# The attention sums of a convolution chain: k stationary in two column halves of the array, put together by one matmul with two identities

## The chip, the cores and the metric

The kernel runs on one core of a Trainium2 chip. The metric is the device time of one execution in microseconds (us), measured over several runs. The kernel is written in a low-level language in which every engine has its own program: TensorE (PE, with its weight loads listed as PEld), VectorE (DVE), ScalarE (ACT), GpSimd (POOL) and SyncE (SP, which issues all DMAs). The programs meet at semaphores. All numbers here are fp32; operands typed F32R are fp32 that TensorE takes in a faster, less exact way. A plain fp32 matmul appears in the trace as two pairs of weight load and matmul; an F32R matmul and a transpose appear as one.

## What is computed

The input x is (8, 64, 64, 48): eight images of 4096 tokens with 48 channels. Four layers follow one another. Only the first has attention, and only its middle is touched here:

```python
xn = (xe - bn_mean) * (bn_gamma * rsqrt(bn_var + BN_EPS)) + bn_beta
q, k, v = split(xn @ w_qkv + b_qkv, 3, axis=2)
q = q - mean(q, axis=2); k = k - mean(k, axis=2)
q2, k2 = q * q, k * k
q2 = _l2n(q2 / (sum(q2, axis=2) + 1e-07), axis=2)
k2 = _l2n(k2 / (sum(k2, axis=2) + 1e-07), axis=1)
kv = einsum('bnc,bnd->bcd', k2, v)
t2 = einsum('bnc,bcd->bnd', q2, kv) / sqrt(N)
attn = (v + t2) @ w_ln + b_ln
```

Then come a 1x1 convolution over attn and the shortcut, a 3x3 convolution (conv2) and a 1x1 convolution (w3), a depthwise and pointwise layer (L1), a layer of mixed experts with its own depthwise convolution (expand, taps, project), and another depthwise and pointwise layer (L3).

## The kernel before

**The attention sums.** v is linear in x, so the kernel never forms kv from v. For each image it forms one matrix over the 4096 tokens, G = [x, k2, 1]' k2, with 97 rows (48 of x, 48 of k2, one of ones) and 48 columns. The rows of x and of ones give kv after a small matmul with prepared weights; the diagonal of the k2 rows gives the norm of k2 over the tokens. The tokens lie in the tile `tok`, 128 partitions by 2 parities (even and odd image rows) by 16 runs by 145 columns (q, x, k, 1). `attention_sums` (L1017) makes 32 matmuls into one bank, over 2 parities and 16 runs, all accumulated: the stationary operand is the 97 columns x, k, 1 of a token group, the moving one its 48 columns of k. Each contracts over 128 tokens.

**What stands around it.** DVE's `sums_out` (L592) waits for `g_done` and copies G to `gt`, and G times a diagonal mask to `gm`. PE's `attention_weights` (L1028) waits for both, and makes two small matmuls (L1032, L1033). From these DVE and ACT make the weights `w1_cur` of conv1 (`conv1_weights`, L599). Before the sums, ACT squares the scores into `tok`, DVE's `norms_begin` (L567) sums the squares, and POOL's `scale_k` (L939) scales k in `tok`; `attention_sums` waits for that (`k_scaled`). DVE's `norms_end` (L582) scales q, and stands in DVE's program ahead of `sums_out`.

**The order of the work.** The images are staged in a software pipeline that is written out by hand: `iteration(f, attn, back)` works on conv2, L1 and the routing of image f, on the attention of image attn = f + 1, and on the project and L3 steps of image back = f - 1. It runs once for f = 0 (no back), in a loop for f = 1 to 6, and once for f = 7 (no attn). Image 0's attention stands ahead of all of them. So six images have their attention sums beside an L3 (f = 1 to 6), and images 0 and 1 have it without one. On PE the order in an iteration is: conv2, project and L1, attention scores (L1013), routing (L1103), l3 in four chunks of 15 matmuls of 512 columns (L1094, L1096, L1097), attention_sums (L1024), out_tokens (16 transposes, L1172), attention_weights, expand_halo (L1109, L1110), and conv1 with expand between its chunks (L1045, L1053, L1109).

`l3` (L1178) fills banks that ACT empties one after another (`l3_out`, L1359, into `outc`). `out_tokens` (L1165) waits for the last of these, and its own results go out through ACT (`tokens_out`, L1365). `expand_halo` (L1112) waits for the mixed weights of DVE's `mix_weights` and for the DMAs of `copy_x2`.

Of all this the change's steps touch `attention_sums`, `sums_out`, the call of `l3`, and the preparation on DVE (L442 to L461).

Of the kernel before, what the change touches and what calls it, by code (L numbers as in the profile page):

```python
# [7 lines left out]
ALU = mybir.AluOpType  # L8
# [4 lines left out]
IMAGES, H, W, C = 8, 64, 64, 48  # L13
# [5 lines left out]
RUN = W // WQ  # L19
# [8 lines left out]
PCHUNKS = HALF // BANK  # L28
ROWS = BANK // W

Q_AT, X_AT, K_AT, TOK = 0, C, 2 * C, 3 * C + 1
# [25 lines left out]
BEHIND = 128 - C2  # L57
APART = C2 - BEHIND

B_COPIES, WT_COPIES, X2_COPIES = 7, 16, 4  # L60
# [55 lines left out]
def conv_chain_kernel(nc, a, out):  # L116

    ctx = ExitStack()
    with ctx:
        def sb(name, shape, dt=F32):  # L120
            return ctx.enter_context(nc.sbuf_tensor(name, shape, dt))

        def sem(name):
            return ctx.enter_context(nc.semaphore(name))
# [32 lines left out]

        s1, s2, u, r = (sb(n, [128, k, 2 * RUN]) for n, k in (("s1", 2), ("s2", 1), ("u", 2), ("r", 1)))
        gt, gm = sb("gt", [SUMS, C]), sb("gm", [SUMS, C])
        rk = sb("rk", [C, 1])  # L160
# [72 lines left out]
        norm_q, norm_k = sem("norm_q"), sem("norm_k")  # L233
        u_ready, q_scaled, k_scaled = sem("u_ready"), sem("q_scaled"), sem("k_scaled")
        gt_ready, w1_ready = sem("gt_ready"), sem("w1_ready")
        xq_ready, y1_slope, y1_max, y1h_ready, y1l_ready, y1l_last = (
# [169 lines left out]
        def token(par, i, at, n):  # L406
            return tok[:, par, i, at:at + n]
# [20 lines left out]
        def _(dve):  # L428
# [21 lines left out]
            step(nc.vector.memset(xq[C2:C2 + 1, :, :], 1.0))  # L450
            step(nc.vector.memset(ones[:], 1.0))

            def fold_norm(inv, shift, gamma, mean, beta):
# [5 lines left out]

            dve.wait_ge(prep_pe, 1)  # L460
            step(nc.vector.tensor_copy(col0[:, :], banks[0][0:C2, 0:Z_ROWS]))  # L461
            step(nc.vector.tensor_scalar_add(inv96[:, L0:L0 + 1], col0[:, Z_VAR:Z_VAR + 1], BN_EPS), "variance")
# [129 lines left out]
            def sums_out(image):  # L592

                bank = ring_a.bank(A_G)
                dve.wait_ge(g_done, image + 1)
                nc.vector.tensor_copy(gt[:, :], bank[0:SUMS, 0:C]).then_inc(gt_ready, 1)
                nc.vector.tensor_tensor(gm[:, :], bank[0:SUMS, 0:C], gram_mask[:, :], ALU.mult).then_inc(gt_ready, 1)

# [361 lines left out]
        def _(pe):  # L960
# [56 lines left out]
            def attention_sums(image):  # L1017

                bank = ring_a.take(pe, image, A_G)
                pe.wait_ge(k_scaled, image + 1)  # L1020
                for par in range(2):
                    for i in range(RUN):
                        first, final = par == 0 and i == 0, par == 1 and i == RUN - 1
                        last = nc.tensor.matmul(bank[0:SUMS, 0:C], token(par, i, X_AT, SUMS), token(par, i, K_AT, C),  # L1024
                                                start=first, stop=final)
                last.then_inc(g_done, 1)

# [149 lines left out]

            def l3(image):  # L1178
                pair_conv(image, L3, ring_d, D_L3, l3_done, range(PCHUNKS))

            def iteration(f, attn, back):
# [26 lines left out]
                if back is not None:  # L1208
                    l3(back)
                if attn is not None:  # L1210
                    attention_sums(attn)
                if back is not None:
                    out_tokens(back)
# [6 lines left out]
            attention_scores(0)  # L1220
            attention_sums(0)
            attention_weights(0)
            conv1(0, None)
# [7 lines left out]
            project(IMAGES - 1, range(PCHUNKS), last_image=True)  # L1231
            l3(IMAGES - 1)
            out_tokens(IMAGES - 1)
# [235 lines left out]
```

## Time and profile before

| what | us |
|---|---|
| median of 3 runs | 1265.95 (1265.3 to 1267.52) |
| the profiled execution's own time | 1266.09 |
| its span, first to last instruction | 1264.3 |
| PE busy with matmuls | 1175.6 (93% of the span) |
| PE busy with weight loads (beside the matmuls) | 756.8 (60%) |
| DVE busy | 892.4 (71%) |
| ACT busy | 475.6 (38%) |
| POOL busy | 119.8 (9%) |
| one iteration in the loop, from one image's sums to the next's | 142.2 |

The profiled execution lies 0.14 us above the median. A line of the views names the source line, the engine, the operation, the tile written and the tiles read, and the shape; for TensorE a form such as 128*97 128x48 is 128 rows by 97 stationary columns, and a moving operand of 128 partitions by 48 columns. PEclk is the clock granted to TensorE as a share of full speed. Matmul durations are modelled from start to the last result, and matmuls overlap, so the time that a row of them takes is read from their starts.

### The profile page before, as it was taken

Reading aid. Unit: us, or ns where it says so; the run is one execution under the profiler, and the core shown is the slowest. Engines: PE = TensorE matmul, PEld = TensorE weight load, DVE = VectorE, ACT = ScalarE, POOL = GpSimd, SP = SyncE. Lnnn points to the kernel's source line nnn. Section 1 sums busy time; section 2 is a strip of 40 time slices with the busy share of each in tenths; the row PEclk is TensorE's granted clock in tenths of the full one; section 3 lists DMA queues with packets and bytes.
Section 4 is the critical chain, followed back from the end, with each engine's and each line's share of the span. In section 5 each row is a group of like instructions: output and inputs, shape, how many; then the busy total and the mean of one; then the engine's idle time right before and its main releaser. Section 6 shows DMA issues by size and latency. Waiting matters only on the chain.

```text
span 1264.3 us, 14703 instructions
## 1 busy us (share of the span) xinstructions
PE 1175.6 (93%) x4981; PEld 756.8 (60%) x4981; DVE 892.4 (71%) x1154; ACT 475.6 (38%) x812; POOL 119.8 (9%) x72
## 2 busy tenths in 40 slices
PE   4789879999999999999999999999999999998986
PEld 3556566646665575656665575656665575655434
DVE  4552359984699459984699459984699459982850
ACT  3211334245532444245532444245532444242421
POOL 0310003000300003000300003000300003000000
PEclk9689869999999999999999999999999999999997
DMA  2011631069113772069113771069113770069016
GB/s 52 21 36 21 81 51 38 1 85 132 45 21 40 100 103 37 0 85 131 44 21 40 100 103 37 0 85 130 45 22 40 101 103 1 1 85 134 25 27 83
DMA packets 183179, 72.91 MB, mean 58 GB/s; under 512 B 174349, under 2 KB 174962, under 8 KB 183154
## 3 DMA queue, kind: packets, MB, share of 16 engines
q1 hardware_dynamic: 183154, 72.58, 41.6%
q8 instruction: 15, 0.25, 0.1%
q14 instruction: 10, 0.08, 0.0%
HBM read 10.51 MB, written 6.29 MB: 13 GB/s over the span
## 4 chain that ended last, share of the span: by engine, by line
PE 80%; DVE 7%; issue 4%; ACT 3%; SPq 2%; DMA 2%; POOL 0%; ACTq 0%; DVEq 0%; POOLq 0%
PE bank L1070 32%; PE bank L1094 8%; PE bank L1024 4%; PE bank L1081 4%; PE bank L1053 4%; PE bank L1160 3%; PE bank L1161 3%; PE bank L1013 3%; DVE dwa L632 3%; PE bank L1097 3%; PE bank L1096 3%; PE bank L1109 2%; PE bank L1138 2%; PE bank L1110 2%; DMA y_parts<-a_parts 2%
## 5 line engine op out<-in xcount | busy, mean ns | idle before, releaser
L1070 PE MATMUL bank<-y_parts,w_h 96*96 96x512 f32 x1152 | 301.8, 411 | 0.0
L632 DVE SCALAR_TENSOR_TENSOR dwa<-h1a,dyn,dwa 128x1024 f32<-128x1024 f32 x240 | 294.0, 1278 | 0.0
L1070 PEld LDWEIGHTS bank<-y_parts,w_h 96*96 96x96 f32 x1152 | 186.6, 163 | 98.5 <-issue 13.2
L632 DVE SCALAR_TENSOR_TENSOR dwb<-h1b,dyn,dwb 128x1024 f32<-128x1024 f32 x128 | 154.9, 1278 | 0.0
L1070 PE MATMUL bank<-y_parts,w_l 96*96 96x512 f32 x576 | 147.9, 401 | 0.0
L1094 PE MATMUL bank<-a_parts,wt_h 128*96 128x512 f32 x384 | 117.4, 415 | 16.4 <-DMA y_parts<-a_parts 15.9
L1070 PEld LDWEIGHTS bank<-y_parts,w_l 96*96 96x96 f32 x576 | 93.4, 162 | 44.3
L949 POOL TENSOR_TENSOR y_parts<-y,y_parts 96x512 fp32r<-96x512 f32 x56 | 96.4, 1725 | 190.5 <-DVE y L672 189.0
L943 POOL TENSOR_TENSOR tok<-tok,u 128x1536 f32<-128x1536 f32 x8 | 22.4, 2796 | 747.3 <-DVE u L573 747.3
L1094 PEld LDWEIGHTS bank<-a_parts,wt_h 128*96 128x96 f32 x384 | 61.5, 166 | 49.6 <-issue 18.7
L713 DVE SCALAR_TENSOR_TENSOR a_parts<-v,a_parts 96x512 fp32r<-96x512 f32 x64 | 43.5, 688 | 52.4 <-ACT a_parts L1339 49.6
L1053 PE MATMUL bank<-xq,w_cur 97*96 97x512 f32 x128 | 69.5, 625 | 9.7 <-DVE y L672 9.7
L670 DVE TENSOR_TENSOR y_parts<-bank,y 96x512 fp32r<-96x512 f32 x64 | 68.5, 1071 | 7.6 <-ACT y L1286 6.7
L1311 ACT ACTIVATE y<-bank,b2s 96x512 f32<-96x512 f32 x32 | 21.9, 683 | 136.3 <-PE bank L1070 136.3
L1311 ACT ACTIVATE xq<-bank,b2s 96x512 f32<-96x512 f32 x32 | 21.9, 685 | 130.9 <-PE bank L1070 122.0
L1024 PE MATMUL bank<-tok 128*97 128x48 f32 x512 | 55.0, 277 | 15.6 <-POOL tok L943 15.6
L1160 PE MATMUL bank<-dwa,pc 128*96 128x512 f32 x128 | 65.4, 592 | 0.0
L1161 PE MATMUL bank<-dwb,pc 128*96 128x512 f32 x128 | 65.3, 592 | 0.0
L1024 PEld LDWEIGHTS bank<-tok 128*97 128x97 f32 x512 | 55.0, 196 | 16.9 <-issue 16.0
L726 DVE TENSOR_TENSOR y_parts<-y,y_parts 96x512 fp32r<-96x512 f32 x32 | 22.1, 689 | 50.8 <-ACT y_parts L1352 50.8
L1094 PE MATMUL bank<-a_parts,wt_l 128*96 128x512 f32 x192 | 57.8, 410 | 0.0
L1362 ACT ACTIVATE dwa<-bank,conv_bias,inv 96x512 f32<-96x512 f32 x32 | 24.8, 774 | 81.4 <-PE bank L1097 81.4
(223 smaller groups left out, 1701.6 us busy)
## 6 DMA issues: line engine op xcount, KB each, us to landing
y_parts<-a_parts SPq DMA_DIRECT2D x32, 396.0 KB, 6.1
y_parts<-a_parts SPq DMA_DIRECT2D x64, 192.0 KB, 6.6
tok<-in_x_dram SPq DMA_DIRECT2D x96, 96.0 KB, 2.6
a_parts<-a_parts SPq DMA_DIRECT2D x32, 264.0 KB, 3.3
x_even<-y_parts SPq DMA_DIRECT2D x16, 384.0 KB, 9.0
x_odd<-y_parts SPq DMA_DIRECT2D x16, 384.0 KB, 7.9
out_dram<-dwb SPq DMA_DIRECT2D x32, 192.0 KB, 2.3
y_parts<-a_parts SPq DMA_DIRECT2D x32, 132.0 KB, 4.3
```

The source lines that it names most:

```text
L632: nc.vector.scalar_tensor_tensor(out=dst, in0=tap_input(n, t), scalar=weight, in1=dst, op0=ALU.mult, op1=ALU.add).then_inc(tap_step, 1)
L670: nc.vector.tensor_tensor(y1_view(y1_h, k - 1), bank_tokens(bank), y1_tokens(k - 1), ALU.max).then_inc(y1h_ready, 1)
L713: return nc.vector.scalar_tensor_tensor(out=lo[:, rows, 1:W + 1], in0=src[:, m % 2, :].rearrange("p (j w) -> p j w", w=W), scalar=0.0, in1 ...
L949: nc.gpsimd.tensor_tensor(y1_view(y1_l, k), y1_tokens(k), y1_view(y1_h, k).bitcast(F32), ALU.subtract).then_inc(y1l_ready, 1)
L1024: last = nc.tensor.matmul(bank[0:SUMS, 0:C], token(par, i, X_AT, SUMS), token(par, i, K_AT, C), start=first, stop=final)
L1053: nc.tensor.matmul(bank[0:C2, :], w1_cur[:, :], xq[:, (k - 1) % 2, :], start=True, stop=True)\
L1070: last = nc.tensor.matmul(bank[0:C2, :], wgt[:, t, :], src[:, rows, cols], start=t + n == 0, stop=t == TAPS - 1 and n == 2)
L1081: last = nc.tensor.matmul(bank[0:C2, :], w3eo[:, par, :], rows[:, :, par, :], start=par == 0, stop=par == 1)
L1094: nc.tensor.matmul(bank[0:C2, :], wgt[layer][:, kw, :], own[:, rows, kw:kw + W], start=n + kw == 0, stop=False)
L1160: nc.tensor.matmul(bank[0:C2, :], pc[:, 0, cols], first[:, :, par, :], start=False, stop=False)
L1161: last = nc.tensor.matmul(bank[0:C2, :], pc[:, 1 + m // 2, cols], other[:, :, par, :], start=False, stop=par == 1)
L1311: nc.scalar.activation(y2[(k // 2) % 2][:, (k % 2) * BANK:(k % 2 + 1) * BANK], ring_c.bank(C_2 + k)[0:C2, :], ACT.Identity, bias=b2s[:, 0: ...
```

## The change

Each of the 32 matmuls now has k (48 columns) stationary and x, k, 1 (97 columns) moving, so that the bank gets the transpose of G. The even tokens write partitions 0 to 47 of the bank, the odd ones partitions 64 to 111: two accumulations side by side, with the matmuls of both parities in turn. DVE copies both halves to the tile `gs` (112 partitions by 97; the 16 between them stay zero). One matmul with `gs` stationary and `twin` moving (two identities of 48 under one another, on partitions 0 and 64) adds the halves and turns them back, into columns 128 to 175 of the same bank. From there `gt` and `gm` are made as before. Between the sums and this gathering matmul stands the last of the four chunks of l3, where there is one.

```diff
+ODD_AT = 64
+APART_ROWS = ODD_AT + C
...
+        gs, twin = sb("gs", [APART_ROWS, SUMS]), sb("twin", [APART_ROWS, C])
...
+        gs_ready, gt_done = sem("gs_ready"), sem("gt_done")
...
             step(nc.vector.memset(ones[:], 1.0))
+            step(nc.vector.memset(gs[:], 0.0))
+            step(nc.vector.memset(twin[:], 0.0))
...
             dve.wait_ge(prep_pe, 1)
+            for at in (0, ODD_AT):
+                step(nc.vector.tensor_copy(twin[at:at + C, :], ident[at:at + C, at:at + C]))
...
                 bank = ring_a.bank(A_G)
-                dve.wait_ge(g_done, image + 1)
-                nc.vector.tensor_copy(gt[:, :], bank[0:SUMS, 0:C]).then_inc(gt_ready, 1)
-                nc.vector.tensor_tensor(gm[:, :], bank[0:SUMS, 0:C], gram_mask[:, :], ALU.mult).then_inc(gt_ready, 1)
+                dve.wait_ge(g_done, 2 * image + 2)
+                for at in (0, ODD_AT):
+                    nc.vector.tensor_copy(gs[at:at + C, :], bank[at:at + C, 0:SUMS]).then_inc(gs_ready, 1)
+                both_parities = bank[0:SUMS, 128:128 + C]
+                dve.wait_ge(gt_done, image + 1)
+                nc.vector.tensor_copy(gt[:, :], both_parities).then_inc(gt_ready, 1)
+                nc.vector.tensor_tensor(gm[:, :], both_parities, gram_mask[:, :], ALU.mult).then_inc(gt_ready, 1)
...
                 pe.wait_ge(k_scaled, image + 1)
-                for par in range(2):
-                    for i in range(RUN):
-                        first, final = par == 0 and i == 0, par == 1 and i == RUN - 1
-                        last = nc.tensor.matmul(bank[0:SUMS, 0:C], token(par, i, X_AT, SUMS), token(par, i, K_AT, C),
-                                                start=first, stop=final)
-                last.then_inc(g_done, 1)
+                for i in range(RUN):
+                    for par, at in enumerate((0, ODD_AT)):
+                        last = nc.tensor.matmul(bank[at:at + C, 0:SUMS], token(par, i, K_AT, C), token(par, i, X_AT, SUMS),
+                                                start=i == 0, stop=i == RUN - 1)
+                        if i == RUN - 1:
+                            last.then_inc(g_done, 1)
+
+            def attention_gather(image):
+
+                pe.wait_ge(gs_ready, 2 * image + 2)
+                nc.tensor.matmul(ring_a.bank(A_G)[0:SUMS, 128:128 + C], gs[:, :], twin[:, :], start=True, stop=True).then_inc(gt_done, 1)
...
                 if back is not None:
-                    l3(back)
+                    l3(back, (0, 1, 2))
                 if attn is not None:
                     attention_sums(attn)
+                if back is not None:
+                    l3(back, (3,))
+                if attn is not None:
+                    attention_gather(attn)
...
             attention_sums(0)
+            attention_gather(0)
```

**The order on PE in the loop.** Before, from the last group of the fourth l3 chunk to the small matmuls of the attention (L81 and L1031 are register instructions):

```order
L1094 MATMUL bank<-a_parts,wt_h 96x512 x3
L1096 MATMUL bank<-y_parts,wt_h 96x512
L1097 MATMUL bank<-y_parts,wt_h 96x512
L81 REGISTER_ALU
L1024 MATMUL bank<-tok 97x48 x32
L1172 MATMUL bank<-ident,dwa 128x96 x16
L81 REGISTER_ALU
L1031 ISA
L1032 MATMUL bank<-wva_aug,gt 48x96
L1033 MATMUL bank<-ones,gm 48x1
```

Now, from the last matmuls of the third chunk on (L1036 is the sums; L1112, L1114 and L1115 are l3):

```order
L1114 MATMUL bank<-y_parts,wt_h 96x512
L1115 MATMUL bank<-y_parts,wt_h 96x512
L84 REGISTER_ALU
L1036 MATMUL bank<-tok 48x97 x32
L1112 MATMUL bank<-a_parts,wt_h 96x512 x3
L1114 MATMUL bank<-y_parts,wt_h 96x512
L1115 MATMUL bank<-y_parts,wt_h 96x512
```

The sums have moved ahead of the fourth l3 chunk. Further on, from the last group of that chunk (L1044 is the gathering matmul, L1190 the transposes of out_tokens, L1050 and L1051 the small matmuls):

```order
L1112 MATMUL bank<-a_parts,wt_h 96x512 x3
L1114 MATMUL bank<-y_parts,wt_h 96x512
L1115 MATMUL bank<-y_parts,wt_h 96x512
L1043 ISA
L1044 MATMUL bank<-twin,gs 97x48
L1190 MATMUL bank<-ident,dwa 128x96 x16
L84 REGISTER_ALU
L1050 MATMUL bank<-wva_aug,gt 48x96
L1051 MATMUL bank<-ones,gm 48x1
```

Where the 32 matmuls of the sums stood, between l3 and the transposes, there is one matmul.

**The order on DVE in the loop.** Before, at `sums_out`:

```order
L589 TENSOR_TENSOR tok<-tok,r 128x32x48
L596 COPY gt<-bank 97x48
L597 TENSOR_TENSOR gm<-bank,gram_mask 97x48
L602 TENSOR_SCALAR rk<-bank 48x1
L604 RECIPROCAL rk<-rk 48x1
```

Now, with the two copies to gs ahead:

```order
L598 TENSOR_TENSOR tok<-tok,r 128x32x48
L606 COPY gs<-bank0 48x97 x2
L609 COPY gt<-bank0 97x48
L610 TENSOR_TENSOR gm<-bank0,gram_mask 97x48
L615 TENSOR_SCALAR rk<-bank1 48x1
```

Nothing else moved on DVE: the copies stand behind the scaling of q, as the copy to gt did.

## Rows read from the trace of the kernel before

**Rows 1.** The page: the chain that ended last, share of the span by engine

```profile
PE 80%; DVE 7%; issue 4%; ACT 3%; SPq 2%; DMA 2%; POOL 0%; ACTq 0%; DVEq 0%; POOLq 0%
```

**Rows 2.** The page: the group L1024 (busy us, mean ns | idle before, releaser)

```profile
L1024 PE MATMUL bank<-tok 128*97 128x48 f32 x512 | 55.0, 277 | 15.6 <-POOL tok L943 15.6
```

**Rows 3.** Timeline of PE and PEld, image 4: start us, us, instructions

```profile
601.11 0.40 PE L1096 MATMUL bank<-y_parts,wt_h 128*96 128x512 f32 x1
601.35 0.40 PE L1097 MATMUL bank<-y_parts,wt_h 128*96 128x512 f32 x1
601.59 5.61 PE L1024 MATMUL bank<-tok 128*97 128x48 f32 x64
607.03 2.35 PE L1172 MATMUL bank<-ident,dwa 96*128 96x96 f32 x16
...
601.11 0.16 PEld L1097 LDWEIGHTS bank<-y_parts,wt_h 128*96 128x96 f32 x1
```

**Rows 4.** Timeline of DVE and ACT, same stretch

```profile
601.27 1.76 DVE L589 TENSOR_TENSOR tok<-tok,r 128x1536 f32<-128x1536 f32 x1
607.24 0.21 DVE L596 COPY gt<-bank 97x48 f32<-97x48 f32 x1 [4.21 <-PE bank L1024]
...
601.79 0.77 ACT L1362 ACTIVATE dwa<-bank,conv_bias,inv 96x512 f32<-96x512 f32 x1 [2.81 <-PE bank L1097]
```

**Rows 5.** Timeline, image 4's scores: matmuls of 192 moving columns

```profile
580.37 1.46 PE L1013 MATMUL bank<-qkw,xcm 97*128 97x192 f32 x8
```

**Rows 6.** Timeline of PE in the preparation: L983 writes two column halves

```profile
64.63 0.24 PE L980 MATMUL bank<-ident,h1a 44*96 44x44 f32 x1
64.70 0.24 PE L981 MATMUL bank<-ident,h1a 52*128 52x52 f32 x1
64.87 0.32 PE L983 MATMUL bank<-ident,h1a 52*64 52x52 f32 x4
```

**Rows 7.** Timeline of the SP queue and landing times of x_odd's DMAs, same iteration

```profile
591.54 5.05 SPq L863 DMA_DIRECT2D x_odd<-y_parts  x2
...
DMA to landing us min/median/max: 6.3/7.6/8.8
```

**Rows 8.** Timeline, image 0: the sums and what follows

```profile
36.17 10.66 PE L1024 MATMUL bank<-tok 128*97 128x48 f32 x64 [7.95 <-POOL tok L943]
...
47.34 0.53 PE L1032 MATMUL bank<-wva_aug,gt 97*48 97x96 f32 x2 [0.51 <-DVE gm L597]
47.66 0.29 PE L1033 MATMUL bank<-ones,gm 97*48 97x1 f32 x2
```

**Rows 9.** Busy by stretch: from:to, length, PE, PEld, DVE, ACT, POOL, PEclk, DMA, GB/s

```profile
36.17:46.50 10.33, 10.33 (x64) 10.33 (x64) 2.61 (x5) 0.23 (x1) 0.00 (x0) 0.50 0.14 30
...
46.50:53.30 6.80, 6.29 (x23) 3.79 (x23) 1.82 (x6) 2.57 (x5) 0.00 (x0) 0.50 0.00 0
180.20:186.40 6.20, 5.77 (x21) 4.85 (x21) 2.77 (x9) 0.20 (x1) 0.00 (x0) 0.50 0.00 0
```

**Rows 10.** Timeline of PEld, image 0: weight loads of the scores

```profile
21.41 1.82 PEld L1013 LDWEIGHTS bank<-qkw,xcm 97*128 97x128 f32 x8 [0.26 <-ACT xcm L1246]
...
23.52 1.27 PEld L1013 LDWEIGHTS bank<-qkw,xcm 97*128 97x128 f32 x8 [0.29 <-ACT tok L1256]
```

**Rows 11.** Timeline, images 1 and 4: from the small matmuls to conv1's first

```profile
180.63 0.53 PE L1032 MATMUL bank<-wva_aug,gt 97*48 97x96 f32 x2 [0.50 <-DVE gm L597]
187.80 1.02 PE L1053 MATMUL bank<-xq,w_cur 97*96 97x512 f32 x2
...
609.31 0.37 PE L1032 MATMUL bank<-wva_aug,gt 97*48 97x96 f32 x2
...
614.10 1.02 PE L1053 MATMUL bank<-xq,w_cur 97*96 97x512 f32 x2
```

**Rows 12.** Timeline, preparation: first wait of DVE, first transposes of x

```profile
7.15 0.16 DVE L461 COPY col<-bank 96x7 f32<-96x7 f32 x1 [1.11 <-PE bank L964]
...
17.84 3.75 PE L1001 MATMUL bank<-ident,tok 128*96 128x128 f32 x16 [2.88 <-DMA tok<-in_x_dram]
```

More of the change, by code:

```diff
@@ L1176, in l1, with l3 @@
                 pair_conv(image, L1, ring_b, B_L1, l1_done, chunks)
-            def l3(image):
-                pair_conv(image, L3, ring_d, D_L3, l3_done, range(PCHUNKS))
+            def l3(image, chunks):
+                pair_conv(image, L3, ring_d, D_L3, l3_done, chunks)
             def iteration(f, attn, back):
@@ L1231, in _ @@
             project(IMAGES - 1, range(PCHUNKS), last_image=True)
-            l3(IMAGES - 1)
+            l3(IMAGES - 1, range(PCHUNKS))
             out_tokens(IMAGES - 1)
```

## The prediction

> **What bounds the kernel now.** I read the chain of waits first. TensorE makes up 80% of the chain that ended last [rows 1], so a microsecond that PE saves is a microsecond of the kernel, unless what follows was waiting for something else. The groups by line then show what the sums are: 512 matmul instructions, 64 per image, busy for 55.0 us [rows 2]. The 15.6 us of idle time ahead of them fall on two images only, and in both POOL's scaling of k ends them. The timeline of image 4 shows one of the six images of the loop. PE goes from the last matmul of l3 (601.35) through the sums without a gap to the first transpose of out_tokens (607.03), which is 5.68 us [rows 3]. The other engines wait there: DVE has waited 4.21 us when the sums end, and ACT has emptied the last l3 bank by 601.79 + 0.77 = 602.56 [rows 4]. So in the loop the sums lie wholly on the path, and so do they in images 0 and 1, where they take 10.66 us at half the clock [rows 8, 9].
>
> **What limits the sums themselves.** 64 instructions in 5.61 us, less some 0.25 for the last one's own length, is a step of 0.085 us. The matmuls of the scores move 192 columns in steps of (1.46 - 0.3) / 7 = 0.165 us [rows 5]. By that 48 moving columns would take 0.04. So the step of 0.085 is that of the weight load, of 97 columns, and not of the moving data. Swapped, a load of 48 columns takes 0.042 by proportion, and 97 moving columns 0.165 x 97 / 192 = 0.083, say 0.084. **The swap alone therefore gains nothing: the step stays at 0.084.** All the gain must come from the two halves running beside each other.
>
> **Do halves run beside each other?** There is one place that shows it. L983 writes partitions 0 to 63 and 64 to 127 with two fp32 matmuls, 4 instructions. They take 0.32 us from the first start to the last end, where one matmul of their size takes 0.24 alone [rows 6]. One after another, with steps of about 0.05 or more for the 64 columns of each load, they would need 0.4. I take it that the halves overlap, though both there read the same moving data, and here each half has its own. So 64 instructions become 32 steps of 0.084, or 2.69 us.
>
> **The loop, six images.** Added: PE changes between full and halved columns twice. From L981 to L983 its step is 0.17 us, from L980 to L981 0.07 [rows 6], so a change costs 0.10, and two cost 0.20. The fourth chunk of l3 is only moved: the same 15 matmuls. But the cover of its ACT step is gone. Before, the sums ran while ACT emptied the bank. Now out_tokens is reached directly behind l3, and waits: 602.56 - 601.35 = 1.21, and some 0.2 for the semaphore, the load and the start of the matmul: 1.4 from the last l3 matmul to the first transpose. The gathering matmul (two instructions with loads of 97 columns, 2 x 0.085 = 0.17) fits into that wait, and costs nothing. It needs `gs`, though. DVE is free at 601.27 + 1.76 = 603.03 [rows 4], two copies of about 0.2 later it is 603.45. PE starts the sums one chunk of l3 (15 steps of 0.238, 3.58 us) earlier, at 597.8, ends them at 600.7, and reaches the gathering matmul one chunk later, at about 604.2. That leaves 0.8 us, and out_tokens can wait another microsecond or so unseen. The sum for one image: 5.68 before, 2.69 + 0.20 + 1.4 = 4.29 now, a gain of 1.39. **Six images give 8.3 us.**
>
> What follows must be ready that much earlier. `gt` and `gm` are made beside out_tokens' transposes, as before. expand_halo at 609.66 waits for the copies of x2. The last was issued by 591.54 + 5.05 = 596.59, and the slowest took 8.8, so all are there by 605.4, over 2 us before the new time of about 608.3 [rows 7]. DVE's, ACT's and POOL's later work in the iteration hangs on conv1 and conv2, which move along.
>
> **Images 0 and 1, half clock.** A step of 96 moving columns is (47.66 - 47.34) / 2 = 0.16 us there [rows 8], so 32 steps of 0.165 make 5.28 instead of 10.56. Here the gathering step has no cover. From the last sums' end (36.17 + 10.66 = 46.83) through DVE to L1032 it is 0.51 us. This path is now walked twice, the first time with two wider copies (0.6), and the gathering matmul lies between, 0.53 as L1032's pair, and 0.1 more for wider loads; the last matmul of the sums is 0.08 longer too. Added: 0.6 + 0.6 + 0.1, about 1.4 with the rest. **Gain 5.28 - 1.4 = 3.9 each, 7.8 in both.**
>
> **The clock in these two images.** It stands at 0.50 all through the sums and through the next 6 us [rows 9]. In the scores of image 0 it rose: eight loads took 1.82 us, and the next eight 1.27 [rows 10]. There 192 columns move per step; in the old sums 48 beside a load of 97. The new sums move 97 in each half, nearer to the scores. If the clock does not rise, the term is nothing. If it rises in the sums and stays, the upper end: some 10 of the 32 steps at half the price, 0.8 us per image, and 0.3 in the waits behind; and what follows runs at full clock. In image 1 this takes 187.80 - 180.63 = 7.17 us, against 614.10 - 609.31 = 4.79 in image 4 [rows 11], 2.4 us; in image 0, with no expand, I put it at half, 1.2. Together 5.8. I take 2.2, the sums' own part alone, because behind them PE waits for DVE for about a microsecond and may lose the clock again.
>
> **Preparation.** Two memsets fall into a wait of 1.11 us on DVE, and two copies of 48x48 (0.4 us with their waits) stand on DVE's chain behind it. PE waits 2.88 us for the DMA of x later on, which hides them [rows 12]. If that cover were gone it would be 0.4 us once.
>
> **The sum.** 8.3 + 7.8 + 2.2 = 18.3 off the profiled execution's own 1266.09 gives 1247.8 us. The median is 1265.95, so nothing is to be corrected. With the clock term at its ends it is 1250.0 or 1244.2.
>
> **A rule against it.** The load of L1097 starts at 601.11, together with the matmul of L1096 on the same 128 rows [rows 3], so loads run beside matmuls on the same rows, and the step of l3 is set by its 512 columns. The Trainium skill (TensorE: Matmul & The Clock Gate, Part 3, "The mechanism") says that a weight load overlaps running matmuls only when the row groups differ; both halves here use all rows. By that rule each pair would take its two loads and then its matmuls, 0.042 + 0.042 + 0.084 = 0.168, and the time would be that of the first rival below, 1276.7 us. The trace speaks against it for the full array. For halves only rows 6 bear on it, and weakly, so this outcome is the first rival.
>
> **The rivals.**
> 1. *The halves take turns* (loads or moving data go through one port). 64 steps of 0.084 are 5.38 us, with two changes of mode and the wait for ACT 6.98 per image against 5.68: a loss of 1.3, 7.8 in the loop. In images 0 and 1 the sums stay at 10.56 and the 1.4 of the gathering is lost, 2.8. Time 1276.7. For it: L983 is one short row with shared data. Against it: that row. The loop turns to a loss from the point where the sums take over 5.68 - 1.6 = 4.1 us, 0.064 per instruction. Chance 0.12.
> 2. *Only the loads are serial*: a pair of instructions takes 0.084 + 0.042 = 0.126, the sums 4.0 us. The loop then gains 0, and images 0 and 1 10.56 - 7.9 - 1.4 = 1.3 each. Time 1263.5. Chance 0.12.
> 3. *The gathering matmul waits for DVE* although the sums are fast: if DVE is 2 us later than above, for lack of the 0.8 us of slack, PE waits some 1 us more in each of six images, 6 us. Time 1253.8. Against it: DVE's place in the order is unchanged, and it stood waiting for 4.21 us. Chance 0.08.
> 4. *The change does nothing*, since the path turns to something that doesn't move, such as the DMAs of x2. Rows 7 leave 2 us, so this is small; chance 0.02, time 1264 or so.
>
> **How the numbers follow.** The forecast has 0.66, and reaches from 1243 to 1252 with its clock term and a microsecond of error. No change means within 0.2%, 2.5 us, about what a measurement of this kernel can tell. Faster by more than that, under 1263.4: the forecast, rival 3 and half of rivals 2 and 4, 0.81. Same: the other half, 0.07. Slower: rival 1, 0.12. The range for 8 in 10 takes in the forecast, rival 3 and most of rival 2: 1243 to 1264.
>
> **What would show it.** In the changed profile the sums' 64 instructions would take 2.7 to 2.9 us in the loop, and about 5.3 or less in images 0 and 1. The transposes of out_tokens would wait about a microsecond for ACT, not the gathering matmul for DVE. The iteration would fall from 142.2 to 140.9 us. PEclk in the sums of image 0 would tell the clock term: 0.5 throughout, or 1.0 from some point on. The prediction is wrong if the sums take over 4 us in the loop.

## The result and the profile after

| | before | after |
|---|---|---|
| median of 19 runs each, us | 1266.23 | 1263.51 |
| lowest to highest, us | 1264.22 to 1267.7 | 1257.03 to 1271.78 |
| profiled execution: time, span, us | 1266.09, 1264.3 | 1264.61, 1262.8 |
| mean granted clock in it | 0.971 | 0.963 |

The ratio is 0.9972, with an interval of 0.9961 to 0.9983. The change makes the kernel faster by 0.28%, 2.7 us. 18.3 us were forecast. The sign was right and the time wrong: 1263.51 is 15.7 us above the forecast of 1247.8. It is just inside the range, whose upper end was drawn for the second rival. That rival's time was 1263.5, the measured one, and this is a coincidence: its sums of 4.0 us were not there (below). The times of the new kernel also scatter over 14.8 us, those of the old one over 3.5. The mean clock goes with them: 0.968 in the run of 1257.03, 0.963 in the one of 1264.61, 0.956 in the one of 1271.78.

The page of the changed kernel, the busy times and the chain (that of before is in [rows 1]), says only that PE still bounds it:

```profile
PE 1161.9 (92%) x4997; PEld 739.7 (59%) x4997; DVE 896.9 (71%) x1174; ACT 476.0 (38%) x812; POOL 119.9 (9%) x72
PE 79%; DVE 9%; issue 4%; ACT 4%; SPq 2%; DMA 2%; POOL 0%; ACTq 0%; DVEq 0%; POOLq 0%
```

**The sums are as fast as forecast.** The timeline of PE, image 4, against [rows 3] (start us, us, instructions):

```profile
594.11 2.88 PE L1036 MATMUL bank<-tok 128*48 128x97 f32 x64
596.92 0.95 PE L1112 MATMUL bank<-a_parts,wt_h 128*96 128x512 f32 x3
...
600.30 0.39 PE L1115 MATMUL bank<-y_parts,wt_h 128*96 128x512 f32 x1
600.53 0.29 PE L1044 MATMUL bank<-twin,gs 112*97 112x48 f32 x2
601.65 2.43 PE L1190 MATMUL bank<-ident,dwa 96*128 96x96 f32 x16 [0.82 <-ACT dwa L1385]
604.01 0.56 PE L1050 MATMUL bank<-wva_aug,gt 97*48 97x96 f32 x2
605.45 0.77 PE L1127 MATMUL bank<-x_even,ew_h 96*128 96x512 f32 x1
611.59 1.02 PE L1071 MATMUL bank<-xq,w_cur 97*96 97x512 f32 x2
```

The 64 instructions take 2.88 us where they took 5.61. The gathering matmul (L1044) starts without a wait behind the last l3 matmul, and the first transpose (L1190) waits 0.82 us for ACT. But from L1050 to the first conv1 matmul L1071 it is now 7.58 us, where it was 614.10 - 609.31 = 4.79 [rows 11]. The windows of busy time show why (from:to, length, PE, PEld, DVE, ACT, POOL, PEclk, DMA share, GB/s):

```profile
594.11:597.00 2.89, 2.89 (x66) 2.76 (x66) 2.65 (x11) 0.77 (x1) 0.00 (x0) 1.00 1.37 99
600.53:603.80 3.27, 2.31 (x19) 2.05 (x17) 0.32 (x2) 1.91 (x4) 0.00 (x0) 1.00 0.00 0
603.80:610.65 6.85, 6.85 (x24) 5.62 (x24) 2.69 (x7) 1.48 (x4) 0.00 (x0) 0.50 0.29 115
317.20:323.90 6.70, 6.70 (x21) 5.25 (x21) 2.46 (x6) 0.79 (x2) 0.00 (x0) 0.50 0.30 117
891.10:897.70 6.60, 6.60 (x36) 4.86 (x35) 3.35 (x8) 2.64 (x6) 0.00 (x0) 1.00 0.30 119
```

The sums run at the full clock. Behind them, at 603.80, the clock falls to 0.50 (1.2 of 2.4 GHz) for 6.8 us, and the small matmuls, the expand and its neighbours go at half speed. The same happens at 317.1, 460.5 and 747.2, but not at 891: in the last row as long a stretch keeps the full clock, and passes 36 instructions where the others pass 21 to 24. The old kernel's clock never fell between image 2's scores and 1152 us.

Read from one image's scores to the next's, the new kernel's periods from image 2 on are 143.70, 143.67, 143.64, 143.58 and 140.75 us; the old one's was 142.25 each time. **A period without a fall is as forecast (140.9). A fall costs 143.65 - 140.75 = 2.9 us, and there were four.** The other stretches of the span: the start +0.4, image 0 from 133.35 to 127.13 (-6.2), image 1 from 141.11 to 140.09 (-1.0), and from the last image's scores to the end 257.2 to 258.45 (+1.3). That last stretch contains the sixth loop image, which should have saved 1.4, so about 2.7 were lost in it. A fall that the old kernel did not have is there, behind the transposes of out_tokens in the last iteration (f = 7):

```profile
1167.00:1173.80 6.80, 5.82 (x16) 4.79 (x17) 2.07 (x4) 2.94 (x10) 0.00 (x0) 0.50 0.30 116
```

Sum: 0.4 - 6.2 - 1.0 + 4 x 1.4 - 1.5 + 1.3 = -1.4 (four periods 1.4 longer, one 1.5 shorter), the difference of the spans to rounding.

Images 0 and 1, against [rows 8, 11]:

```profile
36.84 4.68 PE L1036 MATMUL bank<-tok 128*48 128x97 f32 x64 [7.95 <-POOL tok L956]
42.20 0.37 PE L1044 MATMUL bank<-twin,gs 112*97 112x48 f32 x2 [0.67 <-DVE gs L606]
43.07 0.34 PE L1050 MATMUL bank<-wva_aug,gt 97*48 97x96 f32 x2 [0.51 <-DVE gm L610]
...
163.62 4.45 PE L1036 MATMUL bank<-tok 128*48 128x97 f32 x64 [7.68 <-POOL tok L956]
172.07 0.56 PE L1044 MATMUL bank<-twin,gs 112*97 112x48 f32 x2 [3.99 <-DVE gs L606]
173.13 0.52 PE L1050 MATMUL bank<-wva_aug,gt 97*48 97x96 f32 x2 [0.51 <-DVE gm L610]
```

In both images the sums begin at half the clock and end at the full one. In image 0 it stays up for what follows, until 61.1 (windows):

```profile
36.84:40.60 3.76, 3.76 (x48) 3.76 (x50) 2.61 (x5) 0.23 (x1) 0.00 (x0) 0.50 0.26 48
40.70:44.90 4.20, 2.59 (x34) 2.02 (x31) 1.45 (x7) 0.80 (x2) 0.00 (x0) 1.00 0.03 8
170.30:180.50 10.20, 7.93 (x26) 6.49 (x27) 4.69 (x12) 0.80 (x2) 0.00 (x0) 0.50 0.00 0
```

In image 1 the gathering matmul stands 3.99 us, because DVE has other work until 171.5, and in this wait, at 170.3, the clock falls again (last row). DVE's timeline:

```profile
169.80 1.76 DVE L598 TENSOR_TENSOR tok<-tok,r 128x1536 f32<-128x1536 f32 x1
171.48 0.54 DVE L606 COPY gs<-bank 48x97 f32<-48x97 f32 x2
```

### The profile page after: what moved, and what is told of

Its sections match the earlier page's. It is cut to its first block, busy times and chain, and to the rows that moved or that the text cites. A ratio compares the mean times of both kernels' runs of the same rounds, so it can differ in the third digit from the quotient of the medians.

```text
span 1262.8 us, 14761 instructions
## 1 busy us (share of the span) xinstructions
PE 1161.9 (92%) x4997; PEld 739.7 (59%) x4997; DVE 896.9 (71%) x1174; ACT 476.0 (38%) x812; POOL 119.9 (9%) x72
## 4 chain that ended last, share of the span: by engine, by line
PE 79%; DVE 9%; issue 4%; ACT 4%; SPq 2%; DMA 2%; POOL 0%; ACTq 0%; DVEq 0%; POOLq 0%
PE bank L1088 32%; PE bank L1112 9%; PE bank L1099 4%; PE bank L1071 4%; PE bank L1178 3%; PE bank L1179 3%; PE bank L1026 3%; DVE dwa L645 3%; PE bank L1127 3%; PE bank L1115 3%; PE bank L1114 3%; PE bank L1128 2%; PE bank L1156 2%; PE bank L1036 2%; DVE y_parts L683 2%
## 5 line engine op out<-in xcount | busy, mean ns | idle before, releaser
L1112 PE MATMUL bank<-a_parts,wt_h 128*96 128x512 f32 x384 | 117.5, 415 | 18.3 <-DMA y_parts<-a_parts 18.3
L1112 PEld LDWEIGHTS bank<-a_parts,wt_h 128*96 128x96 f32 x384 | 60.7, 165 | 51.0 <-issue 19.1
L1071 PE MATMUL bank<-xq,w_cur 97*96 97x512 f32 x128 | 68.2, 614 | 10.1 <-DVE y L685 10.1
L1112 PE MATMUL bank<-a_parts,wt_l 128*96 128x512 f32 x192 | 57.3, 407 | 0.0
L1026 PE MATMUL bank<-qkw,xcm 97*128 97x192 f32 x256 | 50.2, 341 | 5.3 <-ACT tok L1279 5.3
L1302 ACT ACTIVATE xq<-bank 96x512 f32<-96x512 f32 x64 | 37.6, 587 | 44.6 <-PE bank L1063 44.6
```

Source lines behind the costliest of these rows:

```text
L1026: last = nc.tensor.matmul(bank[:, m * 2 * C2:(m + 1) * 2 * C2], xcm[:, i * 128:(i + 1) * 128], qkw[:, :], start=True, stop=True)
L1071: nc.tensor.matmul(bank[0:C2, :], w1_cur[:, :], xq[:, (k - 1) % 2, :], start=True, stop=True)\
L1112: nc.tensor.matmul(bank[0:C2, :], wgt[layer][:, kw, :], own[:, rows, kw:kw + W], start=n + kw == 0, stop=False)
```

## The experiments

The theory was now that the stretch between the last l3 matmul and the first expand costs the clock: it holds only narrow matmuls and the new wait, and what comes behind it pays 2.9 us. What makes the stretch is the moved chunk of l3, not the halves. Rival: the halves themselves, their changes of mode or their denser work, make the clock fall. The first four kernels tell the two parts apart.

**e1: the whole of l3 stays ahead of the sums, the gathering follows them directly.**

```diff
-                    l3(back, (0, 1, 2))
+                    l3(back, (0, 1, 2, 3))
                 if attn is not None:
                     attention_sums(attn)
-                if back is not None:
-                    l3(back, (3,))
-                if attn is not None:
                     attention_gather(attn)
```

> The changed kernel, but all four chunks of l3 stand ahead of the sums again, and the gathering matmul directly behind the sums. Theory (the clock): what ate the gain in the loop is a fall of the granted clock to 0.50 for 6.8 us, which follows the 1.1 us wait for ACT, the 16 transposes and the small matmuls. Here the sums cover ACT, and what is left is a wait of 0.6 us of the gathering matmul for DVE; the stretch of little work behind the last dense matmul is shorter, so fewer of the six images show a fall; the iteration is about 140.2 us without one (143.6 with one, in the changed kernel), the time 1248 to 1257. Rival (the halves themselves or the longer path through gs cost the time): the clock has no part in it, the iteration stays near 143, the time near 1263.

1266.74 us (12 runs, 1252.09 to 1269.34), ratio 0.9983 (0.9957 to 1.0008): no difference from before. Image 4 (timeline, then a window):

```profile
598.56 2.88 PE L1036 MATMUL bank<-tok 128*48 128x97 f32 x64
602.11 0.37 PE L1044 MATMUL bank<-twin,gs 112*97 112x48 f32 x2 [0.68 <-DVE gs L606]
605.67 0.77 PE L1127 MATMUL bank<-x_even,ew_h 96*128 96x512 f32 x1
```

```profile
605.20:611.80 6.60, 6.60 (x21) 5.14 (x21) 2.46 (x6) 0.80 (x2) 0.00 (x0) 0.50 0.30 119
```

The expectation failed: there was not a fall fewer, but one in all six images (periods of 143.4 to 143.5). The order is the old one again, but PE now waits for DVE instead of ACT, and from the start of the last of the sums (601.19) to the first 512-column matmul it is still 4.5 us. Two of the twelve runs took 1252.1 and 1252.5, at a mean clock of 0.971 against 0.958 in the profiled one, the slowest of the twelve. Divided over six images, (1269.3 - 1252.1) / 6 is 2.9 us again. That fits a loop without falls, but no trace of such a run was kept, so it is not shown. The same program has both outcomes, and moving the chunk of l3 back is no sure cure so long as a wait stays.

**e2: the order alone.** The kernel before, its sums unchanged, with the fourth chunk of l3 behind them.

```diff
...
-                    l3(back)
+                    l3(back, (0, 1, 2))
                 if attn is not None:
                     attention_sums(attn)
                 if back is not None:
+                    l3(back, (3,))
                     out_tokens(back)
```

> The kernel before, with its old sums, but with the fourth chunk of l3 behind the sums and directly ahead of out_tokens. Theory (the clock): the exposed wait for ACT costs 1.3 us in each of six images, and the clock falls behind it in some or all of them, 2.9 us each: 1274 with none, 1291 with six, and the profile shows stretches of 0.50 in the loop, which the kernel before does not have. Rival (only the halves make the clock fall, by their draw or their form): 1274 and no such stretch.

1286.47 us, ratio 1.0148 (1.0133 to 1.0162): the new order costs the old kernel 20 us. Image 4 kept its clock, image 6 lost it:

```profile
607.22 5.61 PE L1024 MATMUL bank<-tok 128*97 128x48 f32 x64
617.42 2.37 PE L1172 MATMUL bank<-ident,dwa 96*128 96x96 f32 x16 [0.96 <-ACT dwa L1363]
```

```profile
617.50:624.00 6.50, 6.37 (x40) 5.21 (x41) 2.61 (x7) 2.68 (x6) 0.00 (x0) 1.00 0.23 91
907.60:914.30 6.70, 6.70 (x26) 5.43 (x25) 2.69 (x7) 1.26 (x4) 0.00 (x0) 0.50 0.30 117
```

ACT is waited for 0.96 us in every image of the loop. The periods are 146.4 with a fall of 6.8 us, 144.7 with one of 3.4, and 143.4 without. The 143.4 is 1.15 above before. That is the wait for ACT: the 1.4 us of the forecast, from the last l3 matmul to the first transpose, is 617.42 - 616.06 = 1.36 in image 4 (the l3 row is not shown), and 0.24 of it, the step of l3, was there before. The falls are there without any halves, so the rival is out.

**e3: the change, with the wait filled.** Four matmuls of 512 columns stand between the last chunk of l3 and the gathering. Nobody reads their result. Each is typed F32R and so one instruction.

```diff
+            def filler(image, count):
+                bank = ring_a.take(pe, image, A_M2)
+                src = w2_h[:, :, :].rearrange("p t o -> p (t o)")[:, 0:BANK]
+                for _ in range(count):
+                    nc.tensor.matmul(bank[0:C2, :], w2_h[:, 0, :], src, start=True, stop=True)
...
                     l3(back, (3,))
+                if attn is not None and back is not None:
+                    filler(attn, 4)
```

> The changed kernel with four matmuls of 512 columns, whose result nobody reads, between the last chunk of l3 and the gathering matmul in the six images of the loop. They fill 0.95 us in which PE waits for ACT anyway. Theory (the clock): they cost nothing by themselves, and the stretches of 0.50 in the loop become fewer or go; with none the time is 1263.5 less four times 2.9, about 1252. Rival (the clock's fall has another cause, or the falls cost nothing): no change, 1263, or up to 2 us more.

1252.38 us (1251.88 to 1255.22), ratio 0.9894 (0.988 to 0.9909). It does more work than the change and is 11.1 us faster than it. Timeline of image 4, and the window of a whole period:

```profile
592.86 1.09 PE L1046 MATMUL bank<-w_h 96*96 96x512 f32 x4
593.79 0.29 PE L1051 MATMUL bank<-twin,gs 112*97 112x48 f32 x2
593.98 2.37 PE L1197 MATMUL bank<-ident,dwa 96*128 96x96 f32 x16
```

```profile
727.00:868.00 141.00, 137.38 (x619) 87.84 (x617) 110.96 (x136) 59.15 (x100) 14.88 (x8) 1.00 0.47 63
```

There is no fall in the loop, and its periods, from one image's sums to the next's, are 140.76 to 140.80, the forecast's iteration. Three of the four runs lie within 0.8 us; the fourth, 1255.22 at a mean clock of 0.971 against 0.975 and 0.976, has no trace. Only this stretch of PE's work was changed, so what cost the loop its gain is shown: the idle microsecond, not by its length but by the clock behind it.

**e4: the swap alone.** k stationary, both parities in one half, and one copy to gs instead of two.

```diff
-                for at in (0, ODD_AT):
+                for at in (0,):
...
-                    for par, at in enumerate((0, ODD_AT)):
+                    for par, at in enumerate((0, 0)):
...
-                                                start=i == 0, stop=i == RUN - 1)
+                                                start=i + par == 0, stop=i + par == RUN)
...
-                pe.wait_ge(gs_ready, 2 * image + 2)
+                pe.wait_ge(gs_ready, image + 1)
```

> The changed kernel with the swap of the operands, but even and odd tokens both in the first half of the columns, 32 matmuls into one accumulation; one copy to gs instead of two. It shows what the swap does without the halves. Prediction's step: the sums take 64 steps of 0.084 us, 5.4 us in the loop, 2.7 more than with halves; six images and two at the start make about 1285. Rival (the swap alone brings part of the gain, the load being the bound before): sums of under 4.5 us.

1277.45 us, ratio 1.0106 (1.0074 to 1.0137). The sums:

```profile
599.93 5.54 PE L1036 MATMUL bank<-tok 128*48 128x97 f32 x64
```

5.54 against 5.61: the swap alone gains 0.07, as the forecast argued from the two steps. The gain is all in the two halves. Periods are 146.3 (three, with a fall) and 143.4 (two, without). The time is 7.5 us under the 1285 expected, and the four runs differ by 12.4 us, at mean clocks of 0.970 and 0.962. Image 1 holds a surprise. Its sums take 7.03 us, 2.6 more than in the change, and still its period is 137.80 us, 2.3 less than there:

```profile
174.60 0.37 PE L1044 MATMUL bank<-twin,gs 112*97 112x48 f32 x2 [1.12 <-DVE gs L606]
...
176.40:179.80 3.40, 3.40 (x10) 2.49 (x10) 1.62 (x5) 0.00 (x0) 0.00 (x0) 0.50 0.00 0
```

The gathering comes as soon as in the change (22.9 us behind the image's first scores, against 23.2), with less waiting ahead of it, and the stretch at half the clock is 3.4 us long where the change has 10.2.

The next three kernels ask for a cure without useless work, for the way in which the halves overlap, and for images 0 and 1.

**e5: out_tokens cut in two.** The gathering needs DVE, out_tokens needs ACT. Put between two halves of out_tokens, it need wait for neither.

```diff
...
-                    l3(back, (0, 1, 2))
+                    l3(back, (0, 1, 2, 3))
                 if attn is not None:
                     attention_sums(attn)
                 if back is not None:
-                    l3(back, (3,))
+                    out_tokens(back, (0, 1))
                 if attn is not None:
                     attention_gather(attn)
                 if back is not None:
-                    out_tokens(back)
+                    out_tokens(back, (2, 3))
```

> The changed kernel in another order: all of l3, the sums, half of out_tokens' transposes, the gathering matmul, the other half, the small matmuls. Nothing is added. The sums cover ACT's work on the last l3 bank, and the first transposes cover the copies to gs. Theory (the clock): no wait of over a few tenths is left between the sums and the expand matmuls, the stretch without dense matmuls is 3.3 us instead of 4.6, and the clock stays up in the loop as it does in the kernel before; the iteration is 139.6 to 139.9 us, the time about 1246. Rival (the fall hangs on the halved sums, which do not count as work for the clock): stretches of 0.50 in the loop as in the changed kernel, the iteration 142.6, the time 1262.

1245.76 us (1245.51 to 1247.07), ratio 0.984 (0.9827 to 0.9854). Image 4, and a window over almost the whole loop:

```profile
589.63 2.88 PE L1036 MATMUL bank<-tok 128*48 128x97 f32 x64
592.44 1.14 PE L1190 MATMUL bank<-ident,dwa 96*128 96x96 f32 x8
593.41 0.29 PE L1044 MATMUL bank<-twin,gs 112*97 112x48 f32 x2
593.71 1.14 PE L1190 MATMUL bank<-ident,dwa 96*128 96x96 f32 x8
594.77 0.37 PE L1050 MATMUL bank<-wva_aug,gt 97*48 97x96 f32 x2
595.58 0.48 PE L1127 MATMUL bank<-x_even,ew_h 96*128 96x512 f32 x1
```

```profile
310.00:990.00 680.00, 662.70 (x2979) 422.52 (x2978) 541.69 (x647) 285.81 (x480) 71.66 (x39) 1.00 0.46 62
```

No row of image 4 has a wait. The sums' saving of 2.7 arrives nearly whole: periods, again between the sums, of 139.62 to 139.67, 2.6 below before and 1.1 below the change's best. The clock stays up in the whole loop. The order of the change was not needed for the halves, and was its loss.

**e6: the halves in turn.** As the change, but all 32 instructions of one half, then all of the other.

```diff
-                for i in range(RUN):
-                    for par, at in enumerate((0, ODD_AT)):
+                for par, at in enumerate((0, ODD_AT)):
+                    for i in range(RUN):
```

> The changed kernel with the halves one after the other: 16 matmuls of the even tokens in the first half of the columns, then 16 of the odd ones in the second. If PE takes matmuls in the order of the program and overlaps only neighbours, the sums take 64 steps of 0.084 us again, 5.3 us, the iteration 143.4 (146.3 where the clock falls), the time about 1277 as with one half. If its queue reached past 32 instructions, they would stay near 2.7.

1270.46 us, ratio 1.0036 (1.0025 to 1.0046).

```profile
594.58 5.25 PE L1036 MATMUL bank<-tok 128*48 128x97 f32 x64
```

```profile
310.00:1030.00 720.00, 697.92 (x3108) 451.62 (x3107) 557.93 (x685) 295.89 (x500) 74.60 (x40) 1.00 0.47 62
```

5.25 us, 0.29 less than in one half. The steps between single starts are 82 to 87 ns behind the first one, and only at the seam between the halves seven of them are shorter: one of 6 ns and six of 39 to 77. So instructions of different halves overlap only where a few instructions part them: without the alternation in the program the gain is nearly gone. The time is 6.5 us under the 1277 expected, which fits its profile: it showed no fall of the clock in the loop. PE waits 0.82 to 0.83 us for ACT in all six images there, as in e4, whose profile had three falls. The wait alone does not decide, then, and what does is open.

**e7: fillers in images 0 and 1 too.** e3 with 27 and 28 more such matmuls while PE waits for POOL ahead of these images' sums, 12 behind image 1's sums, and four in the last iteration's wait for ACT.

> The kernel with the four filling matmuls, and more of them where PE waits in any case: 27 and 28 ahead of the sums of images 0 and 1, while POOL scales k, 12 behind image 1's sums, while DVE is not yet free for gs, and 4 in the last iteration's wait for ACT. Theory (the clock): the stretches of 0.50 in images 0 and 1 (17 and 17 us long in the run with four) and behind the last out_tokens go; about 1.5 to 2.5 us in image 0, 3 to 4 in image 1 and 3 in the last iteration, together 1252.4 less 8 to 10, 1243. Rival (these stretches lie beside waits for DVE and POOL and cost nothing): 1252.

1249.12 us, ratio 0.9865 (0.985 to 0.988): 3.3 below e3, where 8 to 10 were expected. Images 0 and 1 (two rows of the timeline, then a window):

```profile
37.71 2.88 PE L1036 MATMUL bank<-tok 128*48 128x97 f32 x64 [0.80 <-POOL tok L956]
172.71 0.37 PE L1051 MATMUL bank<-twin,gs 112*97 112x48 f32 x2 [2.63 <-DVE gs L606]
157.00:174.00 17.00, 13.30 (x111) 9.68 (x111) 15.01 (x32) 4.45 (x6) 2.79 (x1) 1.00 0.52 67
```

Around the sums the clock did what was expected, 1.00 through the whole last window, and they take 2.88. But the gathering of image 1 comes no sooner, 23.2 us behind the image's first scores as in e3: DVE is busy for 15.01 of these 17 us, and PE still waits 2.63 us for it. Faster sums are only sooner at that wait.

Cut up like the change, the profiled execution of e7 is 3.0 us shorter than that of e3. The last stretch gives 3.5 (259.02 to 255.50) and image 1's period 1.9 (140.09 to 138.15), where the fall around the gathering lasts 3.4 us instead of 10.2. Image 0's period is 1.4 longer (125.68 to 127.04), with two falls of 10.2 us behind conv1 where e3 has two of 6.8, and 1.1 are lost ahead of its scores, where nothing was changed. In the last iteration the filled wait leaves the clock up. The same window in e3 and in e7:

```profile
1154.80:1161.50 6.70, 6.70 (x18) 5.25 (x18) 2.82 (x5) 1.98 (x7) 0.00 (x0) 0.50 0.30 117
1154.80:1161.50 6.70, 6.28 (x27) 3.79 (x26) 5.06 (x9) 3.94 (x12) 0.00 (x0) 1.00 0.30 117
```

**e8: e5 with these fillers.**

> The split order of out_tokens with the filling matmuls of images 0 and 1 and of the last iteration (none in the loop). If both theories hold, the iteration is 139.6 to 139.9 and the time about 1237; if the split order lets the clock fall, 1253.

1242.49 us (1241.41 to 1243.33), ratio 0.9816 (0.9803 to 0.983): again 3.3 below its base, and 5.5 above the 1237 expected. Between the profiled executions the last stretch is again 3.4 us shorter (258.01 to 254.63), image 0's period 1.6 and image 1's 0.4; its gathering still waits 2.62 us for DVE.

**e9: e5, and in the first iteration DVE copies the sums out ahead of the norms.**

```diff
                 if attn is not None:
-                    norms_end(attn)
-                    sums_out(attn)
+                    if back is None:
+                        sums_out(attn)
+                        norms_end(attn)
+                    else:
+                        norms_end(attn)
+                        sums_out(attn)
```

> The split order, and in the first iteration, where image 1 has its attention and there is no L3, DVE makes its copies to gs, gt and gm ahead of the scaling of q instead of behind it. Theory (in image 1 the gathering matmul waits for DVE, not for the sums): the wait of 4 us there shrinks to 1.5 to 2, and the time is about 2 us under the split order's 1245.8, 1243.5 to 1244.5. Rival (the scaling of q is needed at once by conv1's transposes, so the wait only moves): 1245.8.

1243.22 us (1243.06 to 1244.26), ratio 0.9817 (0.9803 to 0.983), 2.5 below e5.

```profile
168.81 0.37 PE L1048 MATMUL bank<-twin,gs 112*97 112x48 f32 x2 [1.75 <-DVE gs L606]
```

The wait shrinks from 4.02 us in e5 to 1.75: in image 1 it was DVE's order that held the gathering up. But not all of the 2.5 us comes from that. Between the profiled executions image 1's period is only 1.05 shorter (140.11 to 139.06), so the rival, that the wait only moves, holds for a part. The last stretch is 1.9 shorter (258.01 to 256.09), with a fall of 3.4 us behind out_tokens where e5 has 6.8, and image 0's period 0.8, and the edit touches neither.

**e10: e9 with e8's fillers, less the twelve.**

> The same with the filling matmuls ahead of the sums of images 0 and 1 and in the last iteration (none behind image 1's sums). In the split order these were worth 3.3 us. If both effects add, the time is about 1240.5; if the filling had already hidden part of image 1's wait for DVE, 1242.5 as without the new order on DVE.

1241.85 us (1239.26 to 1244.07), ratio 0.98 (0.9786 to 0.9814). It lies between its two expectations. Its median is the lowest, but its interval overlaps e9's, which computes nothing that nobody reads. The gathering of image 1 waits 3.29 us for DVE again, behind sums of 2.88. e9 is the version to keep: 23 us below before, 20 below the change.

## Why the prediction was wrong, and where it was right

- **The halves run beside each other** (2.69 us forecast): right, 2.88 us with the last one's length, 2.64 without. This rules out the first two rivals, the second too, whose time was met by chance. The two changes of mode fit their 0.20: the sums start 0.33 us behind the last l3 matmul, whose step is 0.24, and l3 goes on 0.17 behind the last of them, whose step is 0.08. From rows 6 alone this was weak evidence; e4 and e6 make it firm. The Trainium skill's rule that a weight load overlaps running matmuls only when the row groups differ (TensorE: Matmul & The Clock Gate, Part 3, "The mechanism") would have made it 1276.7 by the forecast's own sum. Two column halves on the same 128 rows overlap here, so the measurement decides against it. e4, where nothing overlaps, came to 1277.45, but with falls of the clock in it.
- **The swap alone gains nothing**: right (e4).
- **The loop, "a gain of 1.39"**: the sum held where the clock held. 140.75 was measured and 140.9 forecast. The 1.4 from the last l3 matmul to the first transpose was 601.65 - 600.30 = 1.35 in image 4, of which 0.82 was waiting, and 1.36 in e2.
- **The failed step** is in the same paragraph, the price of the lost cover: it put down the wait, "1.4 from the last l3 matmul to the first transpose", and put the clock behind it at nothing, without a reason. It counted the wait as idle time and asked what was late next, not what the clock would do. The old stretch from the sums to the expand held the same transposes without a wait; its window in the kernel before was

```profile
606.95:610.20 3.25, 3.12 (x28) 2.84 (x27) 0.49 (x4) 2.08 (x5) 0.00 (x0) 1.00 0.00 0
```

  PE is busy for 3.12 of 3.25 us there, and for 2.31 of 3.27 in the changed kernel at 600.53. Behind the latter the clock falls, in four of six images, for 2.9 us each: 11.6 us. The profiled execution lacks 16.8 us (1264.61 against 1247.8). Beside the four falls these are 4.0 in image 1, 2.7 in the last iteration and 0.4 at the start, less 1.2 that image 0 and 0.5 that the loop's undisturbed sum gave more than forecast. e3 gives the falls back with the wait filled, e5 with the wait avoided. That such a stretch does not always cost the clock is seen in the other two images and in e6; what decides is open. The forecast did have a clock term, and even the sentence that PE "may lose the clock again" beside a wait of a microsecond, but for images 0 and 1 alone. The loop, whose clock had never fallen before, was never asked. The term also counts its own part wrongly: the 2.2 us called "the sums' own part alone" hold 0.6 for the waits behind them.
- **The last iteration** lost about 2.7 us for a fall behind the out_tokens of f = 7. PE's order is unchanged there, and the old kernel has the same wait of 0.96 us for ACT without a fall behind it; e2 and e4 have none either, while e1, e3, e5, e6 and e9 have one. With four matmuls in that wait none follows (e7, e8, e10), and the last stretch is 3.5 and 3.4 us shorter in e7 and e8 than in their bases. That speaks for the same effect as in the loop. Why the old kernel was spared is open.
- **Image 0, gain 3.9 and a share of the clock term**: 6.2 measured. The clock rises within the sums and stays up through conv1. That is the term's upper end, but partly luck: e3 and e1, the same up to there, took 125.68 and 128.09 us for this period where the change took 127.13.
- **Image 1, gain 3.9 and a share of the clock term**: 1.0 measured. "This path is now walked twice" was priced with a free DVE, as in image 0. In image 1 DVE works on mixing the weights and scaling q until 171.5. This is the third rival's mechanism (the gathering matmul waits for DVE), with its own price of 3.99 us, in a place where it had not been looked for; in the loop it did not occur. e9 shows the wait, but wins only 1.05 us in this period by taking 2.3 of it away. Another part is the clock: e4 gained 3.3 here with sums 2.6 us slower than the change's. How the loss divides between the two is open.
- **Preparation at nothing**: the scores of image 0 begin 0.4 us later (21.79 against 21.41). That this is the preparation's price is not shown: in e3, with the same preparation, they begin at 21.37, and in e7 at 22.49.

## What to carry to other kernels

When a cover is removed, look at the granted clock as well as at the wait: here 0.82 us of waiting behind wide matmuls and ahead of narrow ones cost 2.9 more behind it in four of six images, and the same order could come out either way from image to image and run to run. A scatter of the times that was not there before, together with the mean clock, is its mark. When a kernel gets faster, cut its span into periods before giving the edit the credit: in e7 and e9 most of the gain lay where the clock had changed, and in e9 outside the edit. A new step that needs another engine belongs between two pieces of independent work, and its producer's order must be looked at in every iteration, the first one too.

## What the runs showed of the hardware

- Matmuls of two column halves (partitions 0 to 47 and 64 to 111 of the result), both from all 128 rows and each with its own stationary and moving data, overlap when they alternate in the program: 64 instructions (32 fp32 matmuls) in 2.88 us, against 5.54 in one half and 5.25 with the halves in turn. The starts of a pair lie 7 ns apart, and pairs follow each other every 83 ns.
- The clock fell for 6.8 us behind 600.53:603.80, where PE did narrow matmuls and waited 0.82 us, and did not in e3 with four 512-column matmuls in that place. In e6 it did not fall in any of the six images, with the same wait. In the change, e2 and e4, which have both kinds, a period with a fall of 6.8 us is 2.9 to 3.0 us longer than one without, whatever the sums.
- More work on PE can make a kernel faster: e3 against the change, 1252.38 to 1263.51 us, with 24 more matmuls (5021 in its page, 4997 in the change's) that nobody reads.
